# Two window-attention blocks on one core: the table of bias and mask is copied into the banks by ScalarE instead of being multiplied in by TensorE, with new orders of the work

## What is computed

```python
h = roll(layernorm(x), (-3, -3)); split in windows of 49 tokens
q, k, v = h @ qkv_w + qkv_b
attn = (q * scale) @ k.T
attn = attn + bias[head]          # position bias, 49x49 for each head
attn = attn + mask[window]        # 0 or -100, last row and column of windows
o = softmax(attn) @ v
x = x + roll_back(o @ proj_w + proj_b)
m = gelu(layernorm(x) @ fc1_w + fc1_b)
m = layernorm(m)                  # block 0 only
x = x + m @ fc2_w + fc2_b
```

## Time and profile before

| | |
|---|---|
| median of 3 runs | 7130.31 us (7128.76 to 7131.41) |
| the profiled execution | 7130.83 us |
| its span, first to last instruction | 7129.1 us |
| PE busy | 6951.3 us (98%) |
| PE weight loads busy | 5895.1 us (83%) |
| DVE (VectorE) busy | 5031.9 us (71%) |
| ACT (ScalarE) busy | 4674.0 us (66%) |
| POOL (GpSimd) busy | 4523.6 us (63%) |
| mean granted TensorE clock | 0.997 |

### The profile page before, as it was taken

One profiled execution on the slowest core, in us unless ns is written; L12 is line 12 of the kernel. 1 busy time (PEld: TensorE's weight loads), 2 busy tenths in 40 slices (PEclk: granted clock), 3 DMA queues, 4 the chain that ended last, 5 costly groups with the idle time before them and its releaser, 6 DMA issues.

```text
span 7129.1 us, 284978 instructions
## 1 busy us (share of the span) xinstructions
PE 6951.3 (98%) x98848; PEld 5895.1 (83%) x98848; DVE 5031.9 (71%) x18727; ACT 4674.0 (66%) x9220; POOL 4523.6 (63%) x4612
## 2 busy tenths in 40 slices
PE   6999999999999999999999999999999999999999
PEld 5888888888888888888888888888888888888887
DVE  5777777777777777777777777777777777777775
ACT  3666666666666666666666666666666666666665
POOL 3666666666666666666666666666666666666665
PEclk9999999999999999999999999999999999999999
DMA  1111111111111111111111111111111111111111
GB/s 49 47 46 46 46 46 45 46 45 46 45 46 45 46 45 46 45 47 45 47 45 47 45 47 45 47 44 47 44 48 44 48 44 48 43 48 43 48 43 37
DMA packets 604563, 325.43 MB, mean 46 GB/s; under 512 B 450142, under 2 KB 604128, under 8 KB 604320
## 3 DMA queue, kind: packets, MB, share of 16 engines
q1 hardware_dynamic: 604528, 324.96, 17.5%
HBM read 80.71 MB, written 38.54 MB: 17 GB/s over the span
## 4 chain that ended last, share of the span: by engine, by line
POOL 30%; PE 27%; issue 24%; DVE 17%; POOLq 1%; DVEq 0%; SPq 0%; DMA 0%; ACT 0%
POOL hid_sq L956 8%; POOL x_biased L947 7%; PE ps L422 5%; PE ps L526 5%; PE ps L430 5%; POOL hid_ss L958 4%; POOL rstd L967 4%; POOL rstdM L928 4%; PE ps_o L503 3%; PE ps L515 3%; POOL rstdA L928 3%; DVE x_next L890 3%; DVE bnA L801 2%; DVE bnM L801 2%; DVE o_norm L841 2%
## 5 line engine op out<-in xcount | busy, mean ns | idle before, releaser
L928 POOL TENSOR_TENSOR rstdM<-var_epsM,minus_half 98x4 f32<-98x4 f32 x512 | 515.4, 1007 | 1292.6 <-DVE var_epsM L809 1292.6
L830 DVE TENSOR_TENSOR shifted<-ps,negmax 113x392 f32<-113x392 f32 x2048 | 1161.4, 567 | 213.2
L669 ACT ACTIVATE probsT<-ps 98x392 f32<-98x392 f32 x2048 | 952.3, 491 | 431.3 <-PE ps L483 419.7
L928 POOL TENSOR_TENSOR rstdA<-var_epsA,minus_half 98x4 f32<-98x4 f32 x512 | 518.0, 1012 | 1100.0 <-DVE var_epsA L809 1100.0
L826 DVE TENSOR_REDUCE negmax<-ps 113x8 f32<-113x392 f32 x2048 | 1142.7, 558 | 56.4 <-PE ps L471 28.1
L686 ACT ACTIVATE hid<-ps,bfc 128x392 f32<-128x392 f32 x1536 | 873.0, 587 | 416.3 <-PE ps L542 399.2
L662 ACT ACTIVATE probs<-shifted 113x392 f32<-113x392 f32 x2048 | 997.7, 526 | 23.5 <-DVE shifted L830 15.2
L483 PE MATMUL ps<-ident,probs 113*98 113x113 f32 x8192 | 990.7, 264 | 9.2 <-ACT probs L662 7.7
L503 PEld LDWEIGHTS ps_o<-vM,probsT 98*49 98x49 f32 x32768 | 793.8, 125 | 195.6 <-DVE o_norm L841 128.2
L503 PE MATMUL ps_o<-vM,probsT 98*49 98x50 f32 (+1 forms) x32768 | 851.4, 201 | 78.9 <-DVE o_norm L841 78.7
L483 PEld LDWEIGHTS ps<-ident,probs 113*98 113x98 f32 x8192 | 800.9, 129 | 52.8 <-ACT probs L662 9.6
(11 more groups left out here) (99 smaller groups left out, 15077.7 us busy)
## 6 DMA issues: line engine op xcount, KB each, us to landing
kM<-kT SPq DMA_DIRECT2D x512, 85.8 KB
vM<-vA SPq DMA_DIRECT2D x1024, 41.3 KB
vM<-vA SPq DMA_DIRECT2D x1024, 38.3 KB
x_in<-in_x SPq DMA_DIRECT2D x256, 147.0 KB
x_again<-in_x SPq DMA_DIRECT2D x256, 147.0 KB
kM<-kT SPq DMA_DIRECT2D x1024, 36.8 KB
x_keep<-x_next SPq DMA_DIRECT2D x256, 147.0 KB
out_y<-y_out SPq DMA_DIRECT2D x256, 147.0 KB
```

Source lines behind the costliest of these rows:

```text
L669: act.activation(probsT[:, unit_buffer(L, u), :, :, :], free(ps[bank_of[f"T{L}{u}"]][0:PT, 0:1], (SP, 4), (64, 2), (1, TOK)), ACT.Copy).th ...
L830: dve.tensor_tensor(shifted[:, buf, :].rearrange("p (h k) -> p h k", k=TOK), s, free(negmax[:, buf, 0:1], (1, 8), (0, TOK)), ALU.add).then ...
L928: pool.tensor_tensor(rstd[n][:, :], var_eps[n][:, :], minus_half[:, :], ALU.pow).then_inc(s_rstd[n], 1)
```

## The change

`tleft`, `t_high` and the f32r table are gone. The table is now a plain 113 x 6272 array in SBUF with bias plus mask written out for all 113 partitions of a scores bank. A new piece, `seed` (ACT), copies a unit's 392 columns of it into the scores bank, with `ACT.Copy`; there are 8 per body. `scores` then waits for the seeds of all its units, and all its matmuls add (`start=False`). What adds and what overwrites is decided by flags in PSUM that only matmuls set, so: at the start seven matmuls of 452 columns fill the work banks once; every group of matmuls clears flags with its first one only; the uses that filled 384 columns are padded to 392 (`PAD` = 8 columns, in one matmul of `project` and one of `fc2` for L = 1); and a 1x1 matmul on zeros is put ahead of `scores` for L = 0. Mask and bias are loaded as 113 x 6272 and 113 x 3136 floats, in place of two times 98 x 3136 and 6 x 3136, and are added by two VectorE instructions in place of four.

The order is new on every engine, the banks are given out anew, and the pipeline is one body longer (LAST = 5, 261 bodies). The diff, with only the new rows of the lists:

```diff
-LAST = 4
+LAST = 5
...
-        t_high = sb("t_high", [BK, NT], f32r)
-        tleft = sb("tleft", [BK, SP], f32r)
-        table = sb("table", [BK, 2 * NT], f32r)
+        table = sb("table", [SP, 2 * NT])
...
+        BANKS = [("sc00", 1, 5), ("sc01", 1, 3), ("xtM0", 2, 2), ("f1_2_1", 5, 1), ("sc10", 3, 6), ("sc11", 3, 4),
+                 ("sc12", 3, 0), ("f1_0_0", 2, 1), ("f1_1_0", 2, 2), ("f1_2_0", 2, 3), ("f2_1", 5, 1),
...
             def body(i):
+                s0, s1, s3, s5 = Strip(i, 0), Strip(i, 1), Strip(i, 3), Strip(i, 5)
                 load(s0)
+                variants(s1, 0)
+                variants(s3, 1)
+                keep(s3)
                 spread_v(s3, 1)
+                store(s5)
+                load_residual(s1)
+                spread_v(s1, 0)
 
...
+            for bank in ps[:7]:
+                mm = pe.matmul(bank[:, 0:4 * SP], ident[:, :], free(ident[:, 0:1], (0, 4), (1, SP)), start=True, stop=True)
+            mm.then_inc(s_wps, 1)
+
+            def turn(out, x, first, last):
+
+                rows = x.ap[0][1]
+                return pe.matmul(out, x, ident[0:rows, 0:rows], start=first, stop=last, is_transpose=True, skip_group_check=True)
...
-                for u in units:
-                    if free_from := bank_free(x, f"sc{L}{u}"):
-                        pe.wait_ge(*free_from)
-                    if u == units[-1]:
-                        pe.wait_ge(s_qe[L], x.count(1, 1))
-                        pe.wait_ge(s_km[L], x.count(16 * VARIANTS[L], 16 * VARIANTS[L]))
-                    pe.matmul(ps[bank_of[f"sc{L}{u}"]][0:SP, 0:UNIT_COLS], tleft[:, :], table_of(x, L, u),
-                              start=True, stop=False, skip_group_check=True)
+                pe.wait_ge(s_qe[L], x.count(1, 1))
+                pe.wait_ge(s_km[L], x.count(16 * VARIANTS[L], 16 * VARIANTS[L]))
+                pe.wait_ge(s_sd[L], x.count(UNITS[L], units[-1] + 1))
+                if L == 0:
+
+                    pe.matmul(ps[bank_of["sc00"]][0:1, 0:1], ident[:, 1:2], ident[:, 0:1], start=False, stop=True, skip_group_check=True)
...
+                        width = C + PAD if p == PAIRS - 1 else C
+                        mm = pe.matmul(g[0:PT, p * C:p * C + width], oT[L][:, p * PT:(p + 1) * PT], wproj[L][:, 0:width],
+                                       start=(p == 0), stop=(p == PAIRS - 1), skip_group_check=True)
...
             def body(i):
+                s0, s1, s2, s3, s4, s5 = Strip(i, 0), Strip(i, 1), Strip(i, 2), Strip(i, 3), Strip(i, 4), Strip(i, 5)
+                scores(s1, 0, (0, 1))
+                xT(s2, "M0")
+                fc1(s5, 1, 2)
+                scores(s3, 1, (0, 1, 2))
+                fc1(s2, 0, 0)
+                fc1(s2, 0, 1)
+                fc1(s2, 0, 2)
+                fc2(s5, 1)
+                scores(s3, 1, (3, 4, 5))
+                xT(s4, "M1")
+                xT(s0, "A0")
+                probs_turn(s3, 1, 0)
+                fc2(s2, 0)
+                probs_turn(s3, 1, 1)
+                probs_turn(s3, 1, 2)
+                probs_turn(s3, 1, 3)
+                probs_turn(s3, 1, 4)
+                probs_turn(s3, 1, 5)
                 attend(s3, 1, 0)
                 attend(s3, 1, 1)
                 attend(s3, 1, 2)
                 attend(s3, 1, 3)
                 attend(s3, 1, 4)
                 attend(s3, 1, 5)
+                probs_turn(s1, 0, 0)
                 probs_turn(s1, 0, 1)
+                fc1(s4, 1, 0)
                 attend(s1, 0, 0)
                 attend(s1, 0, 1)
                 o_turn(s3, 1)
                 k(s0, 0)
                 o_turn(s1, 0)
                 xT(s2, "A1")
+                fc1(s4, 1, 1)
                 project(s1, 0)
                 k(s2, 1)
+                v(s2, 1)
+                v(s0, 0)
                 q(s0, 0)
                 project(s3, 1)
+                q(s2, 1)
...
+            def seed(x, L, u):
+
+                if x.exists(ns):
+                    if free_from := bank_free(x, f"sc{L}{u}"):
+                        act.wait_ge(*free_from)
+                    act.activation(ps[bank_of[f"sc{L}{u}"]][0:SP, 0:UNIT_COLS], table_of(x, L, u), ACT.Copy).then_inc(s_sd[L], 1)
...
             def body(i):
+                s0, s1, s2, s3, s4, s5 = Strip(i, 0), Strip(i, 1), Strip(i, 2), Strip(i, 3), Strip(i, 4), Strip(i, 5)
+                turned(s2, "M0")
+                gelu(s5, 1, 2)
+                seed(s3, 1, 3)
+                gelu(s2, 0, 0)
+                gelu(s2, 0, 1)
+                gelu(s2, 0, 2)
+                seed(s3, 1, 4)
+                seed(s3, 1, 5)
+                exps(s3, 1, 0)
+                exps(s3, 1, 1)
+                exps(s3, 1, 2)
+                exps(s1, 0, 0)
+                turned(s0, "A0")
+                turned(s4, "M1")
                 exps(s1, 0, 1)
+                exps(s3, 1, 3)
+                probsT_out(s3, 1, 0)
+                exps(s3, 1, 4)
+                exps(s3, 1, 5)
+                probsT_out(s3, 1, 1)
+                probsT_out(s3, 1, 2)
+                probsT_out(s3, 1, 3)
+                probsT_out(s3, 1, 4)
+                probsT_out(s3, 1, 5)
+                probsT_out(s1, 0, 0)
+                probsT_out(s1, 0, 1)
                 gelu(s4, 1, 0)
                 o_out(s3, 1)
+                seed(s2, 1, 0)
                 o_out(s1, 0)
                 turned(s2, "A1")
                 k_out(s0, 0)
+                gelu(s4, 1, 1)
                 k_out(s2, 1)
+                v_out(s2, 1)
+                v_out(s0, 0)
+                q_out(s0, 0)
+                seed(s0, 0, 0)
+                seed(s0, 0, 1)
                 q_out(s2, 1)
+                seed(s2, 1, 1)
+                seed(s2, 1, 2)
...
-                done(dve.tensor_copy(t_high[:, :], t_in[v]))
-                done(dve.scalar_tensor_tensor(out=table[:, half], in0=t_high[:, :].bitcast(f32), scalar=tlow[:, 0:1],
-                                              in1=t_in[v], op0=ALU.mult, op1=ALU.add))
+                done(dve.tensor_tensor(table[:, half], table[:, half], t_in, ALU.add))
...
             def body(i):
+                s0, s1, s2, s3, s4, s5 = Strip(i, 0), Strip(i, 1), Strip(i, 2), Strip(i, 3), Strip(i, 4), Strip(i, 5)
                 stats(s0, "A0")
+                residual(s2, 0)
+                stats(s2, "M0")
+                residual(s4, 1)
+                stats(s4, "M1")
+                shift(s1, 0, 0)
+                low_part(s2, 0)
+                shift(s1, 0, 1)
+                shift(s3, 1, 0)
+                shift(s3, 1, 1)
+                shift(s3, 1, 2)
+                finish1(s5)
+                shift(s3, 1, 3)
+                shift(s3, 1, 4)
+                shift(s3, 1, 5)
+                low_part(s4, 1)
                 third_stats(s2)
                 finish0(s2)
                 stats(s2, "A1")
                 normalise(s3, 1)
                 normalise(s1, 0)
...
             def body(i):
+                s0, s2, s4 = Strip(i, 0), Strip(i, 2), Strip(i, 4)
                 inverse_root(s0, "A0")
+                norm(s0, "A0")
+                inverse_root(s2, "M0")
+                norm(s2, "M0")
+                inverse_root(s4, "M1")
+                norm(s4, "M1")
+                add_bias(s2, 0)
+                squares(s2)
+                add_bias(s4, 1)
                 rstd_of_third(s2)
                 inverse_root(s2, "A1")
                 norm(s2, "A1")
```

187 lines of the change are left out of this document (44 added, 143 removed), and 11 rows, old and new, of the table BANKS.

## The result

The changed kernel takes 7012.26 us (median of 4 runs, 7008.9 to 7013.99) against 7129.89 us (4 runs, 7128.76 to 7131.41) for the kernel before, measured beside it: 0.9834 of it, 95% interval 0.9818 to 0.9849, or 118 us less. The forecast was 325 us less, with a range from 6620 to 6990. So the sign was right, and 207 us of the gain are missing. The profiled execution has a span of 7007.0 us and a mean granted clock of 0.994.

What follows compares the result with a forecast made beforehand. PE's own work was taken as the bound, 26.9 of 27.4 us a body. 25.1 plus waits 0.4, 0.2 and 0.35 gave 26.05; 7130.8 - 256 x 1.35 + 22 = 6807, stated as 6805, range 6620 to 6990.

Steps and rivals of the forecast that it cites:

- Start and end: Outside the loop: larger table loads +10 us, VectorE table instructions -4, fills +4, ramps +17 less 5; together +22 us.
- (a): From `project(s3, 1)` to F: VectorE's chain 5.74 us against 5.3 of PE's work, so PE waits 0.4 us.
- F: Reference point in the loop: the start of `fc1(s2, 0, 2)`, third chunk of fc1 for strip s2, layer 0.
- (b): From F to the first mean matmul of `fc2(s2, 0)`: squares end after 5.74 us, PE's work 5.6, wait 0.2.
- (c): From F to `attend(s1, 0, 0)`: VectorE without a gap 13.5 us, PE 13.1 with (b), wait 0.35.
- 25.1 us of work: PE's own work per body after the change: 27.40 - 0.50 - 1.85 + 0.05, before any new waits.
- Rival 1: In the loop: the forecast waits close and only PE's 25.1 us a body is left, 6564 us; chance 0.14.
- Seeds: ScalarE's eight 113x392 copies, taken at 0.45 us each, 3.6 us a body; ScalarE at 84%.
- Ramps: Pipeline fill and drain outside the loop: 69 us before, +17 for one body more, less 5 as ramps are shorter.
- 2 (a cover fails): In the loop: seeds at 0.55 to 0.7 or K's copies 0.5 late, body 26.4 to 27.0, 6895 to 7050; chance 0.20.
- 3: ScalarE becomes the clock if seeds take over 0.85 us each; at 1.0 us, body 27.95, 7294 us; chance 0.04.
- 4: PE's clock drops from three waits a body; a tenth of its work at 1.2 GHz gives 7447 us; chance 0.02.

Runs made afterwards that it cites:

- run 1: Changed kernel with its two 113-row loads (bias, mask) cut into 112 rows and 1 row each: 6869.9 us, 0.963 of the kernel before.
- run 2: Changed kernel with the residual's four waits reordered, the one for the projection last: 6955.61 us, 0.9752 of the kernel before.
- run 3: Changed kernel with both edits, 113-row loads cut into 112 and 1 and the residual's projection wait last: 6809.66 us, 0.9545 of the kernel before.
- run 10: Kernel of run 3 with the first seed moved on ScalarE behind the copies of oT0, A1 and k0: 6768.8 us, 0.949 of the kernel before.
- run 8: Kernel before's orders, banks and pipeline length, with seeds in place of table passes and the loads of run 1: 7983.49 us, one run.

## Why the prediction was wrong, and where it was right

**The step that failed** is in "Start and end": "By their shapes the table's loads grow from 2.6 to 4.3 MB ... so 1.7 MB more are 10 us". It priced a transfer by its bytes and carried over the rate of the old loads. The rate belonged to the old row counts. Measured: 146 us at PE's first matmul instead of 10, and 5.7 when the same bytes go in rows that divide well. The numbers for a better step were there: the earlier trace rows start at 22.8 behind 3.6 MB, the section on the change tells of loads of 98 rows that become loads of 113, and the rule stands in the page of the Trainium skill that is cited above. I asked how many bytes and not how they are dealt to the engines. No rival covered it, since all four were about the loop. Of the 207 us that are missing, this is 142 (run 1).

**The second miss** is a term of (a): "0.89 until the residual" was read where the wait stood on the addition itself, and measured 1.14 where the changed program has register instructions behind the wait. That is 57 us (run 2). The two add to 199 of the 207, and run 3 shows them together: 6810 where 6805 was forecast. That this is so near is in part luck: inside the body two errors cancel, as below.

**Term by term**, with run 3 where the mends matter:

- The body: forecast 26.05, as it came 26.34, mended 26.09.
- (a), projection to F: forecast 5.74 with a wait of 0.4. Measured 6.01, mended about 5.76. The wait was there: the distance at F is 0.52 (3525.85 to 3526.37) where these passes else follow each other after 0.18, so 0.34.
- (b), F to the first mean matmul: forecast 5.6 of PE's work and 0.2 of wait. Measured 5.87 (3526.37 to 3532.24) without a wait that the rows show. The length is right, the split is not: PE's own work is longer there.
- (c), F to `attend` of layer 0: forecast 13.45, measured 13.44 (3526.37 to 3539.81). Of the wait of 0.35 in it, the gap shows 0.1 at most (3539.54 to 3539.81, less 0.18), and `o_norm` is ready 0.25 us ahead of `attend` (3539.00 + 0.56); in the kernel before, `attend` followed it after 0.05. VectorE isn't what PE waits for there.
- So "25.1 us of work" was about 0.7 too low, hidden by waits that were as much too high: 0.95 forecast, in run 3 0.15 at F and 0.13 at `oT` from start to start. That the two cancel is luck. Run 10 shows it from the other side: its PE is busy 999.99 of 1000 us, with 0.16 left at F, and its body is 25.94. The step behind it is the subtraction 27.40 - 0.50 - 1.85 + 0.05, which takes all the rest of PE's list to cost what it cost in the old order. PE's starts, averaged over the loops, bear out the two terms taken off (0.53 and 1.86); what is left, 25.0 us, takes 25.8 in run 10. The surplus lies in tenths at the hand-overs from one kind of work to another: the projection of layer 1 takes 0.84 us to the start of `q` where it took 0.69 to that of `fc2`, and the 1x1 matmul alone 0.12. Rival 1 (6564) assumed 25.1 to be what is left when the waits close; that time was not to be had.
- Seeds: forecast 0.45 from start to start, measured 0.42 (two in a row last 0.91, one 0.49), and a mean duration of 494 ns. ScalarE forecast at 84% of the loop, measured 81%. The Trainium skill ("ScalarE: Activation LUTs") has ScalarE writing PSUM faster than SBUF; here an exponential of this shape into SBUF has a mean of 520 ns and the copy into PSUM 494, but a copy out of PSUM into SBUF has 491. The functions differ, so this neither bears it out nor speaks against it, and the sum did not hang on it.
- That a moved seed costs something in a place without slack I had looked for only ahead of the scores. It was at `oT`, 0.17 us a body, 41 us in all. The forecast's sum covered it by chance, as a part of the waits that weren't there.
- Ramps: forecast 69 + 17 - 5 = 81, measured 76, and in run 3 84 (6811.5 - 48.2 - 256 x 26.09).

**Rivals.** 2 (a cover fails) was right in kind, a body of 26.34 lies just under its lower edge, but for another reason than its own: no PE wait for a seed or for K's copies comes back in the loop, and the 0.17 at `oT` is a seed that holds back a copy, which no rival named. 3 did not come near: the longest seed took 0.51. 4 did not happen, but run 8, with the same instructions in the old order, has it.

What stays open: between F and `attend` (13.45 us in run 10 too) the rows point to PE's own list, since VectorE is idle for 1.29 us ahead of `finish0` and done with `o_norm` 0.24 ahead of `attend`; no run shortened either engine's work there. Which of PE's new neighbours cost the tenths above, and what the new orders would do with the table passes kept, was not tried.

## What to carry to other kernels

Price a load by its rows as well as its bytes: look at how many of the DMA engines the old shape used (the share column), and see whether the new row count still has a divisor near 16; 113 rows cost 140 us here that 112 + 1 rows did not. When a wait follows a short chain that sets the pace, wait last for what comes last, and look in the compiled order at what stands between that wait and the work. And read a chain from start to start, but don't trust the split of it into work and wait: the sum of mine was right to 0.04 us by chance, with work and waits each wrong by some 0.7, which made a rival look possible that wasn't.
